# Delta-rule attention with experts: a written-out sweep over macro tiles, denser tap operations in the triangular solve, and norms in another place

## The reference, cut to what matters

```python
q = short_conv(x @ Wq, conv_q).reshape(Bx, Tx, H, DK)    # H=8, DK=128, 4 taps, then silu
k = short_conv(x @ Wk, conv_k).reshape(Bx, Tx, H, DK)
v = short_conv(x @ Wv, conv_v).reshape(Bx, Tx, H, DV)    # DV=64
beta = jax.nn.sigmoid(x @ Wb)
g = -jnp.exp(A_log) * jax.nn.softplus(x @ Wa + dt_bias)
# per token: S = S*exp(g); u = (v - k S)*beta; S = S + k u; o = q S   (q, k l2-normalised)
o = gated_delta_rule(q, k, v, g, beta)
o = o * lax.rsqrt(jnp.mean(o * o, axis=-1, keepdims=True) + EPS) * norm_w
o = o * jax.nn.silu((x @ Wg).reshape(Bx, Tx, H, DV))
return o.reshape(Bx, Tx, H * DV) @ Wo
```

## Time and profile before

| | |
|---|---|
| time, median of 3 runs | 2917.67 us (2909.98 to 2919.16) |
| the profiled execution | 2917.61 us, its span 2915.9 us |
| attention from the first elimination (838.0 us) | 2077.9 us, 16 macro tiles |
| granted TensorE clock, mean | 0.926 of 2.4 GHz |
| busy: TensorE, VectorE, ScalarE, GpSimd | 80%, 70%, 43%, 40% of the span |

### The profile page before, as it was taken

The page is one execution under the profiler, slowest core; times in us unless marked ns, Lnnn a source line. Parts: engine busy times, 40 slices in busy tenths (PEclk is TensorE's granted clock), DMA queues, the critical chain, the costliest instruction groups (busy, mean ns, idle before and its releaser), DMA issues.

```text
span 2915.9 us, 97092 instructions
## 1 busy us (share of the span) xinstructions
PE 2319.3 (80%) x36541; PEld 1691.7 (58%) x36542; DVE 2029.1 (70%) x3917; ACT 1256.2 (43%) x3093; POOL 1159.2 (40%) x1152
## 2 busy tenths in 40 slices
PE   4635999999777787879788687879787787879776
PEld 4535999999535464545556364645555464645546
DVE  6672232232268977878787878878887878888885
ACT  0002444443244454455455454545544454555443
POOL 4773444444423342524243342525243342524333
PEclk9997999999889898989898898989898898989998
DMA  5663222222100101011010101011010101011010
GB/s 177 197 217 123 72 72 71 73 72 70 54 23 6 37 7 37 15 27 31 14 38 6 37 7 36 13 30 31 13 38 7 37 7 37 14 28 31 13 29 10
DMA packets 105688, 135.50 MB, mean 46 GB/s; under 512 B 39360, under 2 KB 78816, under 8 KB 105056
## 3 DMA queue, kind: packets, MB, share of 16 engines
q0 software_dynamic: 23552, 61.38, 7.1%
q1 hardware_dynamic: 62448, 40.55, 5.3%
q10 hardware_dynamic: 19312, 28.33, 2.8%
HBM read 76.18 MB, written 54.00 MB: 45 GB/s over the span
## 4 chain that ended last, share of the span: by engine, by line
PE 35%; issue 17%; DVE 11%; ACT 6%; POOL 2%; DVEq 1%; ACTq 0%; DMA 0%; POOLq 0%; SPq 0%
PE att_psA L969 10%; PE att_psS L1087 5%; PE att_psC L969 4%; PE att_psS L1119 3%; DVE att_cv L1378 3%; DVE att_lane_t L1447 3%; DVE att_lanes L1449 2%; PE att_psS L981 2%; PE att_psS L1020 2%; PE att_psA L1010 2%; PE att_psC L1071 2%; ACT att_W L1281 2%; PE att_psC L1050 2%; PE att_psC L1059 1%; DVE att_S L1476 1%
## 5 line engine op out<-in xcount | busy, mean ns | idle before, releaser
L1378 DVE SCALAR_TENSOR_TENSOR att_cv<-att_psA,att_cw,att_cv 128x508 f32<-128x508 f32 (+2 forms) x672 | 474.7, 733 | 103.1 <-ACT att_cv L1218 103.1
L1669 POOL TENSOR_TENSOR att_Sd<-att_S,att_mst 128x1024 f32<-128x1024 f32 x128 | 249.4, 1953 | 716.2 <-DVE att_S L1476 716.2
L969 PE MATMUL att_psA<-att_xt,att_wqkv 128*128 128x512 f32 x896 | 427.2, 621 | 45.2 <-DVE att_cv L1384 29.5
L969 PEld LDWEIGHTS att_psA<-att_xt,att_wqkv 128*128 128x128 f32 x896 | 168.3, 198 | 235.3 <-issue 191.4
L1087 PE MATMUL att_psS<-att_W,att_ktok 128*128 128x128 f32 x2048 | 259.3, 280 | 37.1 <-ACT att_W L1281 21.2
L1087 PEld LDWEIGHTS att_psS<-att_W,att_ktok 128*128 128x128 f32 x2048 | 242.6, 194 | 62.9 <-issue 59.6
L734 PE MATMUL moe_psHT<-moe_xT,moe_w1s 128*128 128x128 f32 x2176 | 267.9, 277 | 0.0
L744 PE MATMUL moe_psY<-moe_w,moe_hT 128*128 x1088 | 258.3, 381 | 0.0
L734 PEld LDWEIGHTS moe_psHT<-moe_xT,moe_w1s 128*128 128x128 f32 x2176 | 256.4, 194 | 0.2
L701 DVE TENSOR_TENSOR moe_y<-moe_psY,moe_b2b 128x256 f32<-128x256 f32 x136 | 57.7, 424 | 273.0 <-PE moe_psY L744 273.0
L675 ACT ACTIVATE moe_hT<-moe_psHT,moe_b1T 128x128 f32<-128x128 f32 x544 | 155.1, 368 | 201.6 <-PE moe_psHT L734 201.6
(11 more groups left out here) (238 smaller groups left out, 4438.8 us busy)
## 6 DMA issues: line engine op xcount, KB each, us to landing
expert_out<-moe_y POOLq DMA_DIRECT2D x136, 128.0 KB, 2.0
route_x_in<-in_L_attn_x_dram SPq DMA_DIRECT2D x64, 128.0 KB
xn_rows<-route_xn ACTq DMA_DIRECT2D x16, 512.0 KB, 3.6
xn_cols<-route_xnT ACTq DMA_DIRECT2D x16, 512.0 KB, 3.1
moe_w<-in_L_ffn_W_dram ACTq DMA_DIRECT2D x2, 4096.0 KB, 24.0
att_xt<-xn_cols SPq DMA_DIRECT2D x16, 512.0 KB, 4.3
att_xr<-in_L_attn_x_dram SPq DMA_DIRECT2D x64, 128.0 KB
out_dram<-att_xr SPq DMA_DIRECT2D x256, 32.0 KB, 1.6
```

What stands on the lines that cost most here:

```text
L969: last = MM(pair_bank(j)[:, h, :], wqkv[:, c, (2 * j + h) * P:(2 * j + h + 1) * P], xt[:, c, :], start=(c == 0), stop=(c == DC - 1))
L1378: V.scalar_tensor_tensor(out=late, in0=by_lane(src[:, h, :])[:, :, 0:LT - d], scalar=cw[:, 2 * j + h, TAPS - 1 - d:TAPS - d], in1=late, op ...
L1669: G.tensor_tensor(new, old, bc(mst[:, par, c, 4 + 2 * two:6 + 2 * two, :], 3, DV), op=ALU.mult).then_inc(s["sd_done" if two else "sd_half" ...
```

## The change

It has three parts. (1) `sweep` loses its hardware loop: the 15 scans that have a next tile are all written out. (2) After every odd step of the elimination two operations of `others` are issued instead of one, so three of them lie beside two steps. (3) `norms(f, 2)` goes ahead of the two `queries` on TensorE, and `squares` of pair 8, which feeds it, goes ahead of `silu` of pair 9 on ScalarE.

```diff
         def sweep(eng, scan, first):
             first()
-            with eng.Fori(0, NG // 2 - 1) as i:
-                for par in range(2):
-                    scan(2 * i + par, par, 2 * i + par + 1)
-            scan(NG - 2, 0, NG - 1)
+            for m in range(NG - 1):
+                scan(m, m % 2, m + 1)
             scan(NG - 1, 1, None)
...
                 norms(f, 1)
                 read_keys(f, par, 0)
+                norms(f, 2)
                 queries(f, par, 0)
                 queries(f, par, 1)
-                norms(f, 2)
...
                 tap3(f, par, 9)
                 silu(f, par, 8)
+                squares(f, par, 8)
                 silu(f, par, 9)
-                squares(f, par, 8)
                 squares(f, par, 9)
...
                     if not alone:
                         next(others, None)
+                        if step[0] % 2:
+                            next(others, None)
                     wait(dve, "elim", INVERT * m + step[0])
```

## The result

The changed kernel takes 2887.36 us (median of 4, 2886.78 to 2888.01) against 2916.17 us before (median of 4, 2909.98 to 2919.16): a ratio of 0.9904, 95% interval 0.9887 to 0.9921, 28.8 us faster. It lies inside the range, 18 us above the forecast of 2869. The forecast move was -48 us, the measured one is -29: the sign came out, the size did not. Of the mechanism, parts 2 and 3 went nearly as forecast; what the loop costs was read too high.

A forecast was written before the change was run, and what follows sets the result against it. Between elimination and scan TensorE was taken as the bound, VectorE during most of the elimination. From 2917.6 us, -58 (loop), +6 (parts 2 and 3) and +4 (last tile) gave about 2869 us, 8-in-10 range 2840 to 2902.

The forecast's parts named there:

- Part 1, -58 us: Sweep loop: writing it out saves 4.5 us in each of 13 looped tiles, 58 us.
- the upper bound: Sweep loop: the whole gap of looped tiles (130.96 us) to two straight ones (126.5), 58 us in all.
- The lower bound: Sweep loop: only six back edges saved, at 3.94 us of TensorE issue each, 24 us.
- only the back edges go: Rival for the sweep: -24 for edges, about -3 for clock, +10 from parts 2 and 3: 2901 us; chance 0.18.
- Part 2, the waits and the last tap: Elimination on VectorE: 2.2 us of new wait at pairs 6 and 7; last tap ends 2.5 us earlier.
- Part 2, links alone: End of elimination: 17 moved links run alone, 0.11 us more each; with other terms it ends 4.3 us later.
- Part 3: hidden: Norms (1.0 us) leave TensorE's way from last silu to read_queries; the moved squares hide behind waits for silu and taps.
- The bound changes to VectorE: Between elimination and scan: elimination ends 59.1 us after its start, behind TensorE's 58.2, and sets the solve; state update at 64.1.
- Parts 2 and 3 together, +10 us: Against straight code: 0.4 us per tile, 6 us in 15 tiles, plus 4 us in the last tile.
- forecast +4: Last tile: nothing is projected, so the elimination's 4.3 us later end comes through, say 4 us.
- Sum: Whole kernel: 2917.6 - 58 + 6 + 4 = 2869.6, about 2869 us.

The follow-up runs named there:

- e9: Only the sweep written out, order of elimination and norms as before, against the kernel before: 2883.6 us, 0.9896.
- e11: Sweep written out and denser elimination, norms and squares left in their old places, against the kernel before: 2882.2 us, 0.9892.
- e8: Full change plus four unused matmuls on TensorE ahead of its wait for the elimination: 2899.9 us, 0.9956 of the kernel before.
- e6: Full change, but two operations beside an odd step only from step 29 on: 2844.3 us, 0.9762 of the kernel before.
- e12: e6 plus six unused matmuls ahead of queries, in TensorE's wait for the last silu: 2836.2 us, 0.9726 of the kernel before.
- e1: Only the sweep written out, on the chip where the kernel before takes 3123.0 us, against that kernel: 3070.4 us, 0.9831.

## Why the prediction was right and wrong, step by step

- **Part 1, -58 us: the step that failed.** The forecast read the loop's cost from two straight tiles, 126.24 and 126.71 us, and took the upper bound "because tile 14 is exactly what each tile becomes". Measured: 31 us (e9). Straight tiles spread over 8 us, in part with the state of TensorE's clock, and those two were short. The lower bound, the edges alone at 3.94 us each, 24 us, was near: the six holes sum to 25.5. Against e9's mean of tiles 1 to 14, 128.6, the looped even tiles of before are 4.0 us longer and the odd ones 1.3, 32 us in twelve tiles; tiles 0, 1, 14 and 15 and a later start take 6 of that back, and the trace of e9 is a long one. So the division by tiles is rough. The rival "only the back edges go", which has 24 us and about 3 for the clock, came nearest for this part.
- **Part 2, the waits and the last tap: right.** New wait 2.2 us (2.3 on average, 5.2 against 2.9), last tap 2.5 us earlier (2.1).
- **Part 2, links alone: right, small by 0.2 us.** The elimination ends 4.6 us later on average, forecast 4.3: 2.3 of waits and 2.3 of links alone, forecast 2.1. The count was off by one: the 50 operations lie beside links 6 to 39, so 16 links move and not 17. A link of 128x238 alone takes 0.43 us, beside a tap 0.31; and the head operation of each pair often follows its last tap directly, 0.83 us start to start instead of 0.65, which I had put at 0.2 us in all. These rows measure 0.12 us per link. The Trainium skill, "VectorE: DVE Perf Modes", section "The DRAIN you can't avoid" (the prediction gives another page's title), measured that a semaphore after each operation costs nothing extra. This case differs, with operations that each read what the one before wrote.
- **Part 3: hidden, as forecast.** With part 2 its place is worth nothing that can be measured (e11); without part 2 it gives 6 to 7 us, within the intervals.
- **The bound changes to VectorE: right, with a price not seen.** The solve starts at T+60.3 on average, right behind the elimination, 0.2 us after it. But the state update comes at T+65.7 on average instead of T+64.1. 1.0 us of that is the elimination's end, T+60.1 instead of T+59.1: I had counted from tile 12, where it ended 0.7 us earlier than on average before, and it moved by 0.3 more. The rest is the clock. In nine of fifteen tiles, the nine in which TensorE waited longest for the elimination, decays and the state product take 1.5 us more, 0.9 us on average (the other steps of this way were some 0.4 shorter than I had them). e8 shows the wait to be the cause: filled, decays are fast in all tiles. VectorE's own wait behind the elimination fell from 7.8 us to 1.4 on average, not to under 1. The trace of before had the sign of it: the clock at 0.50 behind TensorE's waits.
- **Parts 2 and 3 together, +10 us: too high.** By time there is no difference that the intervals tell: 0.9904 and 0.9883 against the 0.9896 of part 1 alone. They were costed against straight tiles with the state update at 63.7; e9 has it at 66.1 in a long trace, the full change at 65.7. That would be -6 us in 15 tiles, and +4.5 in the last tile (129.3 against e9's 124.8; forecast +4): next to nothing.
- **Sum:** -31 and about 0 in place of -58 and +10. The errors, +27 and -10, have one source, the two tiles taken as typical, and the second happened to take back a third of the first. The result would lie inside the range without that too: 2917.6 - 31 + 10 is 2897.

That part 2 costs more than it gives was my theory before the experiments; it fell twice. On the slower chip it gives 21 us, on the others it is neutral. What was left of it, that the links moved in front of pair 7, 7 of the 16, are waste, e6 showed.

## What to carry to other kernels

To interleave more filler into a dependent chain pays only behind the point where the filler's input stops being late; ahead of it the engine waits anyway and the chain's own steps come back at the end, alone and dearer. This hardware loop costs at its back edge, a hole of 3.0 to 4.7 us on TensorE, so four scans in a pass gave what writing all out gave. Do not take one or two periods of a trace as the price of a period: where TensorE's clock falls in some of them, look at all, and ask of every wait that you call hidden what clock TensorE has behind it.

## What the runs showed of the hardware that I had not expected

- Matmuls whose result nobody uses, put in a long wait, raised the granted clock from 0.937 to 0.961 and did not cost time (e12); put in a wait mostly shorter than they are, they cost 20 us, though the clock behind them was as wanted (e8).
- The kernel before takes 2914 to 2916 us beside three of the four sets of runs and 3123 beside the fourth. In the attention there, ScalarE starts the gate of a chunk late in many tiles (in e1 twelve such waits, 57.2 us together). In tile 13 of e1 it sits idle for 5.33 us and starts the gate of chunk 1 at 2697.35, 4.9 us after TensorE is done with it at 2692.4, while GpSimd issues its gathers (ScalarE, and VectorE's wait that follows):

```profile
2690.05 0.60 ACT L1241 ACTIVATE att_gate<-att_psS 128x512 f32<-128x512 f32 x1 [2.26 <-PE att_psS L979]
2690.88 1.14 ACT L1257 ACTIVATE att_ktok<-att_psB,att_mst 128x128 f32<-128x128 f32 x4 [0.23 <-PE att_psB L1037]
2697.35 0.60 ACT L1241 ACTIVATE att_gate<-att_psS 128x512 f32<-128x512 f32 x1 [5.33 <-remote]
...
2702.43 0.75 DVE L1376 SCALAR_TENSOR_TENSOR att_cv<-att_psC,att_cw,att_cv 128x508 f32<-128x508 f32 x1 [7.14 <-ACT att_cv L1216]
```

What releases it, the profile does not name ("remote"), and no run tells the gathers apart from another cause. It stays open, and so does what makes project(4) fall on either side of the clock's change from tile to tile.
